# Three-attention transformer kernel: row maxima of the first and last attention turned by transposing transfers

## The reference

```python
x = x + self_attn(ln(x))      * gate   # 16 heads of depth 16, two windows of 128, rows rolled by 64
x = x + topk_cross(ln(x), ctx) * gate   # 256 x 256 scores, the 16 best keys of each row, softmax over them
x = x + swiglu(ln(x))         * gate   # 256 -> 2048 -> 1024 -> 256
x = x + cross_attn(ln(x), ln(cond rows)) @ Wp + bp    # 16 heads, softmax over all 256 keys
```

## Time and profile before

| | us |
|---|---|
| median of 3 runs | 1279.81 |
| lowest and highest | 1276.47, 1280.52 |
| the profiled execution, its own time | 1284.55 |
| its span, first to last instruction | 1282.4 |
| busy in it: TensorE | 1200.6 |
| VectorE | 1128.0 |
| ScalarE | 1034.6 |
| GpSimd | 855.0 |

### The profile page before, as it was taken

One profiled execution on the slowest core, in us unless ns is written; L12 is line 12 of the kernel. 1 busy time (PEld: TensorE's weight loads), 2 busy tenths in 40 slices (PEclk: granted clock), 3 DMA queues, 4 the chain that ended last, 5 costly groups with the idle time before them and its releaser, 6 DMA issues. The chain is left out here.

```text
span 1282.4 us, 39016 instructions
## 1 busy us (share of the span) xinstructions
PE 1200.6 (94%) x13666; PEld 853.9 (67%) x13666; DVE 1128.0 (88%) x3812; ACT 1034.6 (81%) x2193; POOL 855.0 (67%) x1134
## 2 busy tenths in 40 slices
PE   6778899999999999999999999999999999989987
PEld 6665566667676776767676766767676776656654
DVE  3579999899999999999999989999999999997443
ACT  3745688889898979889797979889797979786764
POOL 1415597959587877859686877959596867776210
PEclk8988999999999999999999999999999999999989
DMA  7542021202121121212021212212121111111111
GB/s 200 149 92 56 22 60 35 63 25 57 39 56 44 47 64 52 57 34 69 21 68 35 64 47 54 58 31 57 28 59 42 47 48 35 43 26 27 26 26 34
DMA packets 111391, 67.25 MB, mean 52 GB/s; under 512 B 13836, under 2 KB 107870, under 8 KB 111198
## 3 DMA queue, kind: packets, MB, share of 16 engines
q1 hardware_dynamic: 109166, 63.71, 19.0%
q10 hardware_dynamic: 2032, 1.05, 0.5%
HBM read 22.33 MB, written 4.19 MB: 21 GB/s over the span
## 5 line engine op out<-in xcount | busy, mean ns | idle before, releaser
L1246 ACT ACTIVATE prob<-turned_score 128x1024 f32<-128x1024 f32 x320 | 325.8, 1018 | 78.5 <-PE turned_score L908 76.1
L1521 POOL TENSOR_TENSOR pair<-full,pair 128x512 f16<-128x512 f32 x182 | 210.9, 1162 | 118.2 <-ACT pair L1201 113.6
L1405 DVE MATCH_REPLACE8 rest<-top,score 128x256 f32<-128x256 f32 x512 | 208.9, 417 | 0.0
L1419 DVE MATCH_REPLACE8 far<-best,rest 128x256 bf16<-128x256 f32 x512 | 206.4, 412 | 0.0
L1402 DVE MAX8 top<-score 128x8 f32<-128x256 f32 x512 | 193.9, 421 | 13.2 <-PE score L908 12.4
L1527 POOL TENSOR_SCALAR far<-far 128x512 bf16<-128x512 bf16 x256 | 158.6, 620 | 41.4 <-DVE far L1419 20.9
L1392 DVE TENSOR_REDUCE rowmax_l<-score 128x4 f32<-128x1024 f32 x121 | 147.8, 1221 | 30.4 <-PE score L908 24.3
L908 PE MATMUL work<-pair_n,w_m_hi 128*128 128x256 f16 x1024 | 173.5, 273 | 0.3 <-ACT full L1194 0.2
L908 PE MATMUL work<-pair_n,w_m_lo 128*128 128x256 f16 x512 | 139.6, 273 | 0.0
L1201 ACT ACTIVATE pair<-full 128x512 f16<-128x512 f32 x192 | 121.1, 631 | 20.2 <-DMA k_stack_l<-pair 1.8
L908 PEld LDWEIGHTS work<-pair_n,w_m_hi 128*128 128x128 f16 x1024 | 96.1, 98 | 19.1 <-issue 7.6
(11 more groups left out here) (212 smaller groups left out, 3206.8 us busy)
## 6 DMA issues: line engine op xcount, KB each, us to landing
k_stack_t<-pair SPq DMA_DIRECT2D x96, 64.0 KB, 2.5
k_stack_l<-pair SPq DMA_DIRECT2D x96, 64.0 KB, 2.6
q_stack_w<-pair SPq DMA_DIRECT2D x93, 64.0 KB, 2.6
k_stack_w<-pair SPq DMA_DIRECT2D x93, 64.0 KB, 2.6
q_stack_t<-pair SPq DMA_DIRECT2D x93, 64.0 KB, 2.6
q_stack_l<-pair SPq DMA_DIRECT2D x93, 64.0 KB, 2.6
ctx_t<-in_ctx_turned SPq DMA_DIRECT2D x16, 256.0 KB, 2.9
ctx_l<-in_ctx SPq DMA_DIRECT2D x16, 256.0 KB, 3.1
```

The costliest lines, as they stand in the source:

```text
L1246: act.activation(prob[:, at:at + 2, :], both_b[:, :, :], ACT.Exp).then_inc(exp_done, 1)
L1405: m = dve.match_replace(rest[p % 2][:, t, :], eight[:, t, :], bank[:, t * L:(t + 1) * L], -FAR)
L1419: m = dve.match_replace(far[p % NFAR][:, t, :], best[p % 2][:, t, :], rest[p % 2][:, t, :], -FAR)
L1521: pool.tensor_tensor(pr[:, 1, :, :], whole[:, :, :], pr[:, 0, :, :], ALU.subtract).then_inc(split_lo, 1)
```

## The change

For w and l the maxima are written as fp16 into a tile of 128x128, whose other columns are zero. A transposing transfer within SBUF (new piece `gx`, on SyncE) turns the whole tile into `turned_max_*`, and `gg` sends its first 8 rows on to the 49th partition. The sign moves into `k_stack_*`, whose 49th partition now holds -1. There are 60 `gx` for w (elements 1 to 15) and 60 for l (elements 0 to 14); element 0 of w and element 15 of l keep TensorE and ScalarE, as does all of t. The lists of all engines are new: `pe` and `act` lose 120 entries each (`gd` and `gc`), `sp` gains 120, `dve` and `pool` keep their number in another order. `IDLE_WORK` rises from 474 dummy matmuls to 600. The number of groups is a table now (`GUARDS`), with 4 everywhere.

```diff
+GUARDS = {"w": 4, "t": 4, "l": 4}
+EDGE_GUARDS = {("w", 0): 4, ("l", 15): 4}
...
+def by_transfer(s, b):
+
+    return s != "t" and (s, b) not in EDGE_GUARDS
...
-        "b_l:5:1 gd_l:5:1 bk_l:4 m1:6:6 a_t:7:7 b_t:7:4 m1:6:7 o_l:5 gd_l:5:2 a_w:9 b_t:7:5 gd_t:7:3 pr_l:4 "
-        "a_w:9:1 o_t:7:2 b_t:7:6 gd_w:9 a_w:9:2 m2:6 gd_w:9:1 a_t:8 b_t:7:7 m2:6:1 m2:6:2 b_l:5:2 m2:6:3 a_l:5:6 "
-        "b_w:9 o_t:7:3 xt_m:6 gd_w:9:2 b_l:5:3 a_w:9:3 ot_t:7 o_w:9 a_l:5:7 b_w:9:1 bk_t:7 o_l:5:1 a_t:8:1 "
-        "b_w:9:2 gd_w:9:3 x4_n4:6 b_l:5:4 o_w:9:1 pr_t:7 o_w:9:2 a_t:8:2 b_w:9:3 pj_lk:6 xt_t:7 b_l:5:5 gd_t:8 "
...
+        "b_t:7:5 gd_t:7:3 a_w:9 pr_l:4 a_w:9:1 o_t:7:2 b_t:7:6 a_w:9:2 m2:6 a_t:8 b_t:7:7 m2:6:1 m2:6:2 a_l:5:6 "
+        "b_l:5:2 m2:6:3 b_w:9 o_t:7:3 xt_m:6 a_w:9:3 b_l:5:3 ot_t:7 o_w:9 b_w:9:1 a_l:5:7 bk_t:7 o_l:5:1 a_t:8:1 "
+        "b_w:9:2 x4_n4:6 b_l:5:4 o_w:9:1 pr_t:7 a_t:8:2 gd_t:8 o_w:9:2 b_w:9:3 pj_lk:6 xt_t:7 o_w:9:3 b_l:5:5 "
...
-        "xi:11 in_tk:8 gg_t:7:2 gg_l:5 in_wk:9 in_tq:8 gg_t:7:3 gg_w:9 gg_w:9:1 gg_l:5:1 ct:9 gg_w:9:2 gg_l:5:2 "
-        "gg_w:9:3 gg_t:8 in_lk:6 gg_l:5:3 in_lq:6 gg_t:8:1 in_wq:10 in_wk:10 xo:4 cl:8 gg_t:8:2 gg_l:6 ct:10 "
...
+        "in_wk:9 gg_l:5:1 in_tq:8 gg_t:7:3 gx_w:9 gx_l:5:2 gg_w:9 gx_w:9:1 gg_w:9:1 xo:4 gx_w:9:2 gg_l:5:2 "
+        "gg_w:9:2 gx_w:9:3 xi:12 gg_w:9:3 gx_l:5:3 gg_l:5:3 gg_t:8 in_lk:6 in_lq:6 gg_t:8:1 in_wq:10 in_tk:9 "
...
-        rowmax = {s: [sb(f"rowmax_{s}{i}", [P, 8], F32) for i in range(2)] for s in "wl"}
-        guard = {s: [sb(f"guard_{s}{i}", [8, P], F16) for i in range(2)] for s in "wtl"}
+        edge_rowmax = [sb(f"edge_rowmax{i}", [P, 8], F32) for i in range(2)]
+        rowmax = {s: [sb(f"rowmax_{s}{i}", [P, P], F16) for i in range(2)] for s in "wl"}
+        turned_max = {s: sb(f"turned_max_{s}", [P, P], F16) for s in "wl"}
...
+                elif kind == "gx":
+                    each = (8 if s == "w" else 16) // groups(s, b)
+                    sp.wait_ge(a_free, a_unit(s, b, each * (i + 1) - 1))
+                    if guard_no(s, b, i) > 0:
+                        sp.wait_ge(guard_in[s], 16 * guard_no(s, b, i))
+                    sp.dma_start(turned_max[s][:, :], rowmax[s][turned_no(s, b, i) % 2][:, :], transpose=True).then_inc(rowmax_turned[s], 16)
+                elif kind == "gg" and by_transfer(s, b):
+                    many = H // 2 // groups(s, b)
+                    sp.wait_ge(rowmax_turned[s], 16 * (turned_no(s, b, i) + 1))
+                    sp.dma_start(stack[s][b % NS[s]]["q"][NR:64 + NR + 1:64, many * i:many * (i + 1), :],
+                                 turned_max[s][0:4 * many, :]).then_inc(guard_in[s], 16)
...
+                    if by_transfer(s, b):
+                        dve.wait_ge(rowmax_zeroed, 1)
+                        if i % each == 0 and turned_no(s, b, g) >= 2:
+                            dve.wait_ge(rowmax_turned[s], 16 * (turned_no(s, b, g) - 1))
+                        maxima = rowmax[s][turned_no(s, b, g) % 2]
...
+            for s in "wl":
+                for one in rowmax[s]:
+                    m = pool.memset(one[:, :], 0.0)
+            m.then_inc(rowmax_zeroed, 1)
             pool.memset(ident32[:, :], 0.0).then_inc(const, 1)
```

More of the change, by code:

```diff
@@ L54, with groups, turned_no, guard_no @@
 BY_TWO = {"wk": 0, "wq": 0, "tq": 0, "lq": 15}
+GUARDS = {"w": 4, "t": 4, "l": 4}
+EDGE_GUARDS = {("w", 0): 4, ("l", 15): 4}
+def groups(s, b):
+    return EDGE_GUARDS.get((s, b), GUARDS[s])
+def by_transfer(s, b):
+    return s != "t" and (s, b) not in EDGE_GUARDS
+def turned_no(s, b, g):
+    return sum(groups(s, one) for one in range(b) if by_transfer(s, one)) + g
+def guard_no(s, b, g):
+    return sum(groups(s, one) for one in range(b)) + g
 ORDERS = {
     "pe": (
[129 rows of a table removed]
-    "act": (
[100 rows of a table removed]
-    "dve": (
[19 rows of a table removed]
[118 rows of a table added]
+    "act": (
[89 rows of a table added]
+    "dve": (
[19 rows of a table added]
         "t2:4:11 t1:4:12 t1:4:13 t2:4:12 rm_l:2:2 t2:4:13 rm_l:2:3 rm_l:2:4 nv_l:1 rm_l:2:5 bn_n1:7 t1:4:14 "
[3 rows of a table removed]
[3 rows of a table added]
         "t1:5:12 t1:5:13 t2:5:12 rm_l:3:2 t2:5:13 rm_l:3:3 rm_l:3:4 nv_l:2 rm_l:3:5 bn_n1:8 t1:5:14 t1:5:15 "
         "t2:5:14 rm_w:7 t2:5:15 rm_w:7:1 xa_l:2 rm_w:7:2 t1:6 t1:6:1 bn_nc:5 rm_l:3:6 t2:6 rm_w:7:3 xa_m:4 nv_t:5 "
[9 rows of a table removed]
[9 rows of a table added]
         "t2:8:7 t1:8:8 xa_w:9 t1:8:9 t2:8:8 rm_l:6 t2:8:9 t1:8:10 t1:8:11 t2:8:10 rm_l:6:1 t2:8:11 t1:8:12 "
         "t1:8:13 t2:8:12 rm_l:6:2 t2:8:13 rm_l:6:3 rm_l:6:4 nv_l:5 rm_l:6:5 bn_n1:11 t1:8:14 t1:8:15 t2:8:14 "
[3 rows of a table removed]
[3 rows of a table added]
         "t1:9:12 t1:9:13 rm_l:7:2 t2:9:12 rm_l:7:3 t2:9:13 rm_l:7:4 nv_l:6 rm_l:7:5 bn_nc:9 t1:9:14 t1:9:15 "
[30 rows of a table removed]
-    "pool": (
[88 rows of a table removed]
-}
-IDLE_WORK = ("pj_wq:0:0=59 gd_w:0:0=30 gd_w:0:1=21 gd_w:0:2=11 bk_w:0:0=17 x4_n2:0:0=25 pj_tq:0:0=38 a_w:1:0=13 "
-             "a_t:0:0=16 a_w:1:2=35 o_w:1:0=14 gd_t:0:1=27 b_t:0:3=7 gd_t:0:2=9 o_t:0:2=11 a_t:1:0=11 pr_w:2:0=12 "
-             "a_l:13:7=10 ot_l:13:0=8 xt_m:15:0=6 x4_n4:15:0=5 a_l:15:1=15 a_l:15:3=11 a_l:15:7=16 bk_l:15:0=14 "
-             "pr_l:15:0=33")
[30 rows of a table added]
+    "pool": (
[99 rows of a table added]
+}
+IDLE_WORK = ("pj_wq:0:0=59 a_w:0:0=30 gd_w:0:1=21 gd_w:0:2=11 bk_w:0:0=17 x4_n2:0:0=25 pj_tq:0:0=38 a_w:1:0=12 "
+             "a_t:0:0=10 a_w:1:2=47 a_t:0:1=32 a_w:1:3=27 b_t:0:1=17 pr_w:1:0=21 gd_t:0:2=6 x4_n2:1:0=40 "
+             "a_w:2:1=16 b_t:0:6=11 b_t:0:7=5 o_t:0:2=19 bk_t:0:0=5 o_w:2:2=14 b_w:2:3=13 a_t:1:3=6 x4_n3:15:0=5 "
+             "xt_m:15:0=5 x4_n4:15:0=30 a_l:15:7=11 bk_l:15:0=14 pr_l:15:0=33")
 def idle_work():
@@ L538, in build @@
         half_bias = sb("half_bias", [P, HC], F32)
-        ones = sb("ones", [33, L], F16)
+        minus_ones = sb("minus_ones", [33, L], F16)
         last_bias = sb("last_bias", [33, C], F16)
@@ L588, in build @@
         top8 = [sb(f"top8_{i}", [P, 2, 2, LT, 8], F32) for i in range(2)]
-        rowmax = {s: [sb(f"rowmax_{s}{i}", [P, 8], F32) for i in range(2)] for s in "wl"}
-        guard = {s: [sb(f"guard_{s}{i}", [8, P], F16) for i in range(2)] for s in "wtl"}
+        edge_rowmax = [sb(f"edge_rowmax{i}", [P, 8], F32) for i in range(2)]
+        rowmax = {s: [sb(f"rowmax_{s}{i}", [P, P], F16) for i in range(2)] for s in "wl"}
+        turned_max = {s: sb(f"turned_max_{s}", [P, P], F16) for s in "wl"}
+        edge_guard = [turned_max[s] for s in "wl"]
+        guard = {"w": edge_guard, "t": [sb(f"guard_t{i}", [8, P], F16) for i in range(2)], "l": edge_guard}
         values = {s: sb(f"v_{s}", [P, LT, H * STEP + SLOT - STEP], F32) for s in "wtl"}
@@ L668, in build @@
         guard_out = {s: sem(f"guard_out_{s}") for s in "wtl"}
+        rowmax_zeroed = sem("rowmax_zeroed")
+        rowmax_turned = {s: sem(f"rowmax_turned_{s}") for s in "wl"}
         stat_done = {s: sem(f"stat_{s}") for s in LN if s not in SUMMED}
@@ L757, in unit, with guard_before @@
             return i // 2, i % 2
+        def guard_before(n, s):
+            b = max(one for one in range(B) if guard_no(s, one, 0) <= n)
+            return d_no["gd_" + s, b, n - guard_no(s, b, 0)]
         def heads(g):
@@ L786, in d_freed @@
             if kind == "gd":
-                return guard_out[s], NG * b + i + 1
+                return guard_out[s], (guard_no(s, b, i) if s == "t" else i) + 1
             if kind == "ot":
@@ L850, in _ @@
                             for one in stack[group]:
-                                sp.dma_start(one["k"][NR:64 + NR + 1:64, :, :], ones[0:H, :]).then_inc(filled, 16)
+                                sp.dma_start(one["k"][NR:64 + NR + 1:64, :, :], minus_ones[0:H, :]).then_inc(filled, 16)
                     if load_no[i] >= NSTAGE:
@@ L878, in _ @@
                         sp.dma_start(rows, src).then_inc(in_stack[s], 16)
+                elif kind == "gx":
[9 more added lines that the diff above has]
+                                 turned_max[s][0:4 * many, :]).then_inc(guard_in[s], 16)
                 elif kind == "gg":
-                    n = NG * b + i
-                    sp.wait_ge(guard_out[s], n + 1)
+                    n, many = guard_no(s, b, i), H // 2 // groups(s, b)
+                    sp.wait_ge(guard_out[s], (n if s == "t" else i) + 1)
                     if n > 0:
                         sp.wait_ge(guard_in[s], 16 * n)
-                    sp.dma_start(stack[s][b % NS[s]]["q"][NR:64 + NR + 1:64, 2 * i:2 * i + 2, :],
-                                 guard[s][n % 2][:, :]).then_inc(guard_in[s], 16)
+                    sp.dma_start(stack[s][b % NS[s]]["q"][NR:64 + NR + 1:64, many * i:many * (i + 1), :],
+                                 guard[s][n % 2][0:4 * many, :]).then_inc(guard_in[s], 16)
                 elif kind == "xo":
@@ L1007, in _ @@
                 elif kind == "gd":
```

(42 more changed lines are left out.)

## The result

The changed kernel takes 1284.09 us (median of 12 runs, 1281.08 to 1288.41) against 1279.17 us for the kernel before (12 runs on the same chip, 1275.87 to 1282.70). The ratio is 1.0042, with an interval of 1.0025 to 1.0058: slower by 0.4%, where a gain of 1% was forecast. The time is inside the range (1250 to 1302), the sign is the other one. The profiled execution has a time of 1282.08 us and a span of 1280.3, less than the profiled execution of before (1284.55); single executions of either kernel are up to 7 us apart, so the sign comes from the repeated runs, and the profiles only say where time lies.

What follows compares the result with a forecast made beforehand. TensorE was taken to bind in the middle (97.9% busy), VectorE close behind and binding before it. 1284.6 - 21.6 + 5.4 + 3 = 1271.4 us, or 1267 off the median; range 1250 to 1302.

Steps and rivals of the forecast that it cites:

- What comes through of TensorE's time: Middle stretch: eight gd a pass at 0.22 us each go, freeing 21.6 us (bounds 10.8 and 34).
- What VectorE lets through: Middle stretch: VectorE has room, at 97.5%, but mutual waits with TensorE give back a quarter, 5.4 us.
- The price of the fp16 output: VectorE's maxima, written as fp16 instead of fp32: no change, from 412 against 417 ns for another operation.
- ScalarE's part: Eight copies of 0.256 us a pass go, 31 us in all; counted as nothing, since ScalarE has 12% idle.
- the bank's relief: Turned groups no longer hold one of three work banks until copied; counted inside the quarter kept.
- SyncE and the transfers: Transposing transfers land in 2.6 us (1.8 to 7.6), issue in 0.6 us each; covered in the middle, no cost.
- rival (a): Transfer latency shows in each pass from a landing of 3.8 us on: slower, 1301 us at 4.5; chance 0.24.
- the sum of 57 us of 70: SyncE's time per pass: 36.7 us plus 4.8 issuing, 10.6 landing waits and 5 guard waits; it fits.
- Ends: Head and tail, where TensorE idles and latency counts: 3 us lost, bounds 0 and 8.
- The sum: Whole kernel: 1284.6 - 21.6 + 5.4 + 3 = 1271.4, a gain of 13.2 us; 1267 off the median.
- Rival (b): No change, 1277 to 1283 us: VectorE and ScalarE, or new order and ends, take the gain; chance 0.13.

Runs made afterwards that it cites:

- old_order_no_turning: Kernel before with its old lists, all turning left out (no gd, gc or gx; gg sends a constant tile): 1270.0 us, ratio 0.9935.
- before_less_tensor: Kernel before with the third term of the MLP's first product left out, 32 matmuls an element fewer: 1270.9 us, ratio 0.9926.
- before_both_less: Kernel before with row maxima of w and l over half the keys and the MLP's first product in two terms: 1267.7 us, ratio 0.9901.
- two-copy run: Changed kernel with each transposing transfer replaced by two plain copies of 64 partitions each: 1284.9 us, ratio 1.0046.

## Why the prediction was wrong

**What comes through of TensorE's time** is the step that failed first. The forecast was 21.6 us freed in the middle, a quarter given back, 16 us gained. The pieces were priced about rightly: 97 `gd` with a slot of 0.11 us and, in the row of `turn`, 9 us of "issue" gaps that go with them (24.4 us in 92 before, 15.5 in 61 in the old lists without turning) make 20 us. The gap had been taken from the row of the turned scores, a different one, and half of it by a guess, so its size is luck. But without any turning the old lists win only 8.3 us over the whole kernel (6 to 11), 0.07 us for each of the 120 `gd`, ScalarE's copies included. The prediction took a busy share of 97.9% to mean that TensorE's work sets the pace nearly one for one. It doesn't: in old_order_no_turning its waits for others in the middle rise from 66.9 to 88.9 us, about as much as was freed. before_less_tensor prices the same: 56 us taken, 9.5 won. The share itself says less than it seems: a busy time of 273 ns stands for a slot of 109.

**What VectorE lets through**, a quarter given back, is the same error a second time. I had looked for the one engine that would bind next; before_both_less shows none among TensorE and VectorE. The mutual waits were read from one row each, 13.9 and 13.7 us; over all rows TensorE waited 29.6 us for ScalarE and 28.0 for VectorE, and VectorE 30.7 for TensorE. The forecast of 97% for VectorE failed accordingly (95.4%).

**The price of the fp16 output** was right at zero, 1221 against 1222 ns. **ScalarE's part** and the bank's relief lie within the 8.3 us; no run tells them from TensorE's.

**SyncE and the transfers.** The landing was right in kind and a little too long (2.2 for 2.6 us), so rival (a), which needed T = 3.8 us, did not come about in the new lists. Against it I had put that every 64 KB transfer between SBUF tiles landed within 3.8 us; that was one kind of stack, and others took up to 5.5 (`k_stack_w`). Each issue was mis-sized: 1.11 us, not 0.6, so a pass has 8 x 0.5 = 4 us more on SyncE. Yet the sum of 57 us of 70 was too high: by the waits of the changed kernel SyncE is busy or between pieces for 44 us of a pass of 71 and waits 5 for landings of `gx` (10.6 had been counted) and 2.5 for guards (5), 51 in all. It fits, as forecast, and the step from there to "no cost" was the error, the second step that failed: transfers were put at nothing and cost 5 to 7 us. A queue in a fixed order doesn't have to be full to be late, since its pieces have due times. The two-copy run shows 6 us lost against no turning, with this issuing time and nothing transposed, in short waits for guards, for buffers of maxima and for an unrelated stack. I had named those queued stacks as the place to look, and counted nothing for them. The mechanism of (a), latency that shows, is real where lists aren't fitted to it: 80 us in the old ones.

**Ends.** 3 us, bounds 0 and 8, was meant for late guards. The new order lost 8 us against the old one, both without turning: in the profiled executions 9.0 us before 290 us, 4.6 won back in the middle, 4.8 lost after it. The step had no term for a new order by itself, the third thing missing. Its cause stays open.

**The sum** by what the runs give: -8.3 for the turning, +8 for the new lists, +5 to +7 for the transfers, which is +5 to +7 against the +5 measured. The terms are differences of the same runs, so this closes by itself and proves nothing; it says only how the 18 us between the gain of 13 that was forecast and the loss of 5 divide: 8 too much from TensorE, 5 for the order beyond the 3 at the ends, 5 for the transfers. Rival (b), with "the new order and the ends give it back" and a `gd` of 0.11 us, had the right parts but for the transfers' cost; it ended at no change, and 0.13 was too little for it.

No run here that does the whole work is faster than the kernel before. With free turning the new lists give 1277.9 us, the old ones 1270.

## What to carry to other kernels

In a kernel whose engines follow fixed lists, with three of them above 85% busy in the middle, take work from one engine and measure how much comes through before pricing a change by its busy time; here it was a sixth on TensorE and a thirtieth on VectorE, and the rest turned up as waits for the other engines. Price a new order of the lists as a change by itself, by running it with the mechanism taken out. A transfer has two prices, its landing and the time it holds the queue that issues it (1.11 us here); the second falls on everything behind it. A test that is to tell them apart has to change one and keep the other, counted to the landing of the last part.

## What was not expected of the hardware

- A transposing transfer of a 128x128 fp16 tile within SBUF held SyncE for 1.11 us (median of 60, least 1.09); a plain copy of the same tile held it for 0.53 us.
- Its landing, 2.2 us after the issue began, was 0.4 to 0.5 us behind the plain copy's 1.8, no more than the time that it held SyncE longer (0.58 us).
- The 120 of them added 19200 packets under 512 B (33036 against 13836), 160 each. A plain copy of the tile has 144, two copies of its halves 160: the small packets come with a tile of 128 rows of 256 B, and 17280 of them in plain copies cost nothing that can be told.
- The reduction of 128x1024 fp32 scores took 1221 ns with fp16 output and 1222 with fp32.
